# Cross-attention and a quantised FFN on one core: the last four row tiles in an order of their own, a second output bank, and the FFN weights in four transposing reads

## What is computed

```python
q = (layernorm(x) @ Wq).heads(); k = (ctx @ Wk).heads(); v = (ctx @ Wv).heads()
a = softmax(q @ k.T * 64**-0.5) @ v
x = x + a @ Wo + bo
def act_q(y, clip):                       # one scale for the whole tensor
    s = sigmoid(clip) * max(abs(y)) / 127
    return clip(round(y / s), -128, 127) * s
def w_q(w):                               # one scale for each row
    s = max(abs(w), axis=1) / 127
    return clip(round(w / s), -128, 127) * s
n  = act_q(layernorm(x), clip_x)
h  = act_q(silu(n @ w_q(w_gate).T) * (n @ w_q(w_up).T), clip_down)
x  = x + h @ w_q(w_down).T
```

## Time and profile before

| | |
|---|---|
| runs, us | 563.13, 563.48, 565.64; median 563.48 |
| profiled execution, us | 564.18; its span, first to last instruction: 562.4 |
| PE busy | 533.8 us (95% of the span) |
| PE weight loads, beside it | 354.2 us (63%) |
| DVE busy | 471.0 us (84%) |
| ACT busy | 293.3 us (52%) |
| POOL busy | 234.8 us (42%) |
| DMA | 93.82 MB, queue of SP 47.9% of 16 engines |

### The profile page before, as it was taken

One profiled execution on the slowest core, in us unless ns is written; L12 is line 12 of the kernel. 1 busy time (PEld: TensorE's weight loads), 2 busy tenths in 40 slices (PEclk: granted clock), 3 DMA queues, 4 the chain that ended last, 5 costly groups with the idle time before them and its releaser, 6 DMA issues.

```text
span 562.4 us, 7992 instructions
## 1 busy us (share of the span) xinstructions
PE 533.8 (95%) x2691; PEld 354.2 (63%) x2699; DVE 471.0 (84%) x874; ACT 293.3 (52%) x408; POOL 234.8 (42%) x352
## 2 busy tenths in 40 slices
PE   4999889999999999999789899999999999899997
PEld 1978668787888878787668644444444446343443
DVE  2747888999989898998987699999989988879883
ACT  3744546556555655544343555555554543999300
POOL 3576748769596876856542000000000000055441
PEclk9999999999999999999999999999999999999999
DMA  8717465765667574536294928750343130399987
GB/s 307 262 41 265 120 201 156 229 211 173 201 224 240 183 238 145 168 98 197 62 295 174 286 45 297 268 160 13 103 113 74 39 76 2 114 339 217 114 110 117
DMA packets 82338, 93.82 MB, mean 167 GB/s; under 512 B 46609, under 2 KB 49425, under 8 KB 82041
## 3 DMA queue, kind: packets, MB, share of 16 engines
q1 hardware_dynamic: 77973, 85.44, 47.9%
q0 software_dynamic: 4320, 7.87, 9.6%
q10 hardware_dynamic: 4, 0.00, 0.0%
HBM read 47.51 MB, written 37.78 MB: 152 GB/s over the span
## 4 chain that ended last, share of the span: by engine, by line
PE 46%; issue 34%; DVE 13%; DMA 5%; ACT 1%; POOL 1%; SPq 0%; POOLq 0%; DVEq 0%
PE QO L194 6%; PE QO L196 5%; PE QO L195 5%; PE SP L382 4%; PE WOP L495 3%; PE WOP L493 3%; PE WOP L494 3%; DMA out<-n2b 2%; PE PTP L1088 2%; PE QO L1088 2%; PE SP L1088 2%; PE PTP L430 2%; DVE P L401 1%; DVE mx L394 1%; DVE x L519 1%
## 5 line engine op out<-in xcount | busy, mean ns | idle before, releaser
L45 POOL DMA_DIRECT2D out<-n2b x30 | 30.2, 1039 | 213.8 <-DVE n2b L1099 213.8
L989 ACT ACTIVATE sil<-QO,fsc 128x512 f32<-128x512 f32 x88 | 60.5, 687 | 72.9 <-PE QO L983 72.9
L983 PE MATMUL QO<-nT,wgu 128*128 128x512 bf16 x352 | 90.4, 379 | 1.0 <-ACT nT L221 0.6
L983 PE MATMUL SP<-nT,wgu 128*128 128x512 bf16 x352 | 90.3, 379 | 0.0
L993 DVE SCALAR_TENSOR_TENSOR h<-SP,fsc,sil 128x512 f32<-128x512 f32 x88 | 65.9, 749 | 10.6 <-PE SP L983 10.4
L422 POOL TENSOR_TENSOR PN<-P,rs 128x512 f32<-128x512 f32 x64 | 44.3, 713 | 57.1 <-DVE rs L414 57.1
L996 DVE TENSOR_REDUCE hmx<-h 128x1 f32<-128x512 f32 x88 | 60.4, 686 | 3.0
L405 ACT ACTIVATE P<-P,r 128x616 f32<-128x616 f32 x32 | 25.9, 811 | 69.7 <-DVE P L401 69.7
L983 PEld LDWEIGHTS QO<-nT,wgu 128*128 128x128 bf16 x352 | 34.3, 98 | 42.7 <-DMA nT<-qb 1.1
L983 PEld LDWEIGHTS SP<-nT,wgu 128*128 128x128 bf16 x352 | 34.4, 98 | 41.5
L194 PE MATMUL QO<-xTs,wqs 128*128 128x512 f32 x128 | 52.0, 406 | 2.9 <-DVE xTs L225 2.6
(11 more groups left out here) (169 smaller groups left out, 1125.9 us busy)
## 6 DMA issues: line engine op xcount, KB each, us to landing
xTr<-in_xT SPq DMA_DIRECT2D x8, 1024.0 KB, 7.6
xn<-in_x SPq DMA_DIRECT2D x32, 256.0 KB, 3.8
out<-x SPq DMA_DIRECT2D x32, 256.0 KB, 2.9
n_rows<-n SPq DMA_DIRECT2D x32, 256.0 KB, 2.6
n2b<-n_rows SPq DMA_DIRECT2D x32, 256.0 KB, 3.9
out<-n2b POOLq DMA_DIRECT2D x30, 256.0 KB, 4.5
h_spill<-h SPq DMA_DIRECT2D x2, 2816.0 KB, 9.4
h<-h_spill SPq DMA_DIRECT2D x6, 768.0 KB, 8.0
```

Of the source, the lines that this page charges most:

```text
L983: m = e.matmul(ps, wv_[:, k, col:col + 128], nT[:, b % 2, :, k, :], start=(k == 0), stop=(k == 3))
L989: t_sil[n] = add("act", lambda e: e.activation(sil[:, n % SR, :], gp, ACT.Silu, scale=fsc[:, ic:ic + 1]), [t_g[n], t_fs, t_h.get(n - SR)] ...
```

## The change

- From step 28 on `attend` is no longer called. A function `last_batch` lists the work of tiles 28 to 31 in another order: `S(29)` and `S(30)` together, `S(31)` behind `wo(24)`, and `PT(30)` and `PT(31)` together. Row tile 30 has its scores and its transposes in `QO` instead of `SP` and `PTP`.
- Output tiles alternate between banks `WOP` and `MI`, in all batches; 30 and 31 use `PTP` and `SP`.
- The transposing read of the FFN weights is cut into four, each of 128 columns: two are listed behind step 27, two behind the loads of the last batch's values.
- The `dg` products go from DVE to ACT, behind `normed(26)`; their matmuls go behind `wo(31)`, into `QO`; the copy to `sdb` goes to ACT behind `normed(31)`.
- The first `keep_clock` has 8 matmuls instead of 20.
- `largest(24)` to `largest(29)` are listed two for each pass of the last loop.

```diff
+        def S_bank(n):
+            return QO if n == 30 else SP
         def S(n):
+            if n == 30:
+                free = [t_oss[6, 0], t_oss[6, 1]]
+            else:
+                free = [t_sub[29] if n == 31 else t_sub.get(n - 1)]
-            t_S[n] = add("pe", fn, [t_q[b], *t_kl, t_sub.get(n - 1)] + ...
+            t_S[n] = add("pe", fn, [t_q[b], *t_kl, *free], "S_mm")
...
         def PT(n):
+            free = t_sub[30] if n == 30 else t_pl[29] if n == 31 else t_pl.get(n - 1)
...
         def wo_bank(n):
-            return {28: PTP[:, 0:512], 29: SP[:, 0:512], 31: SP[:, 512:1024]}.get(n, WOP[:, :])
+            return {30: PTP[:, 0:512], 31: SP[:, 0:512]}.get(n, (WOP, MI)[n % 2][:, :])
         def wo(n):
-            free = t_x1.get(n - 1) if n < 28 else (t_pl[31], t_oss[7, 2], t_x1[27], t_oss[7, 3])[n - 28]
+            free = {30: t_pl[31], 31: t_oss[7, 2]}[n] if n >= 30 else t_x1.get(n - 2)
...
+        def load_wgu(k):
+            c.dma_turn(wgu[:, :].rearrange("p (k n) -> p k n", k=4)[:, k, :], wgud[:, k * 128:k * 128 + 128],
+                     [t_qh[7, 3], t_ws[24], t_ws[25]], "ld_wgu")
+        def last_batch():
...
+            PT(28)
+            S(29)
+            S(30)
+            PT_high(28)
+            soft_max(29)
+            soft_sub(29)
+            load_vb(7)
+            load_wgu(2)
+            load_wgu(3)
+            soft_exp(29)
+            soft_max(30)
+            soft_sub(30)
+            PT_low(28)
...
+            wo(24)
+            S(31)
...
+            wo(25)
+            residual(24)
+            PT(29)
...
+            wo(26)
...
+            PT(30)
+            PT_high(30)
+            PT(31)
+            PT_high(31)
...
+            wo(27)
+            residual(26)
+            PV_rest(7)
+            second(25)
+            residual(27)
+            largest(22)
+            for j in range(4):
+                PV(7, j)
+                if j == 0:
+                    normed(25)
+            second(26)
+            second(27)
+            largest(23)
+            normed(26)
-        for s in range(32):
+        for s in range(28):
             attend(s)
...
+            if s == 27:
+                load_wgu(0)
+                load_wgu(1)
+        last_batch()
...
         for n in range(28, NT):
             wo(n)
             normed(n - 1)
...
-            if n > 28:
-                largest(n - 2)
+            if n < 31:
+                largest(2 * n - 32)
+                largest(2 * n - 31)
...
+        t = add("pe", spread_scale, [t_dg, t_oss[7, 1]], "sd_mm")
+        t_sdb = copy("act", sdb[:, :], QO[:, 512:1024], [t], "sdb")
...
-            keep_clock(20 if which == 0 else 8)
+            keep_clock(8)
```

More of the change, by code:

```diff
@@ L832, in load_n2 @@
                 t_nl[b, tt] = dma("sp", n2b[:, b % 2, tt, :], n2d[4 * b + tt], waits, f"ld_n2b{b % 2}{tt}")
[L834 to L842, removed]
@@ L844, in block_kernel, with second @@
-        for s in range(32):
+        def load_wgu(k):
+            c.dma_turn(wgu[:, :].rearrange("p (k n) -> p k n", k=4)[:, k, :], wgud[:, k * 128:k * 128 + 128],
+                     [t_qh[7, 3], t_ws[24], t_ws[25]], "ld_wgu")
+        def last_batch():
+            def second(n):
+                second_stats(n)
+                second_aggr(n)
+                second_scale(n)
+            normed(22)
+            first_stats(31)
+            first_aggr(31)
+            first_scale(31)
+            wo(23)
+            residual(23)
+            PV_rest(6)
+            second(23)
+            for j in (2, 3, 0, 1):
+                PV(6, j)
+            PT(28)
[11 more added lines that the diff above has]
+            PT_low(28)
+            soft_exp(30)
+            normed(23)
+            soft_sum(29)
+            soft_rec(29)
+            soft_norm(29)
+            wo(24)
+            S(31)
+            soft_sum(30)
+            soft_rec(30)
+            soft_norm(30)
+            soft_max(31)
+            soft_sub(31)
+            soft_exp(31)
+            wo(25)
+            residual(24)
+            PT(29)
+            PT_high(29)
+            soft_sum(31)
+            soft_rec(31)
+            soft_norm(31)
+            PT_low(29)
+            wo(26)
+            residual(25)
+            second(24)
+            largest(21)
+            first_bias(31)
+            PT(30)
+            PT_high(30)
+            PT(31)
+            PT_high(31)
+            normed(24)
+            PT_low(30)
+            PT_low(31)
+            state["free"][0] = state["free"][1] = (t_pl[30],)
+            wo(27)
[12 more added lines that the diff above has]
+            normed(26)
@@ L849, in block_kernel @@
                 t_flat = [t_v[4], t_v[3], t_wol, ("qo_mm", c.count["qo_mm"])]
[L850 to L877, removed]
+            if s == 27:
+                load_wgu(0)
+                load_wgu(1)
+        last_batch()
+        t_wgu = ("ld_wgu", c.count["ld_wgu"])
+        gone = [t_S[31], t_q[7]]
+        for r in range(4):
+            dgt = wraw[:, 0, r * 128:r * 128 + 128]
+            t_dg = add("act", lambda e, r=r, dgt=dgt: e.activation(dgt, identF[:, :], ACT.Identity,
+                                                                   scale=wsc[:, 22 + r:23 + r]),
+                       [t_idF, t_wsc[25], t_wb[24], t_wb[25]], "dg")
         for n in range(28, NT):
@@ L891, in block_kernel, with spread_scale @@
         largest(31)
-        load_n2(1, gone[:2] + [t_n2s[4 + tt] for tt in range(4)])
+        load_n2(1, gone + [t_n2s[4 + tt] for tt in range(4)])
+        def spread_scale(e):
+            for r in range(4):
+                m = e.matmul(QO[:, 512 + r * 128:640 + r * 128], ones[:, :], wraw[:, 0, r * 128:r * 128 + 128],
+                             start=True, stop=True)
+            return m
+        t = add("pe", spread_scale, [t_dg, t_oss[7, 1]], "sd_mm")
+        t_sdb = copy("act", sdb[:, :], QO[:, 512:1024], [t], "sdb")
         add("act", lambda e: e.activation(warm[:, :], sge[:, :], ACT.Silu), [t_sge], "warm")
```

52 lines of the change are left out of this document (23 added, 29 removed).

## The result

| | before | after |
|---|---|---|
| median of 19 runs each, us | 563.48 (562.33 to 565.64) | 560.04 (557.22 to 562.35) |
| ratio, 95% interval | | 0.9935 (0.9923 to 0.9947) |
| profiled execution, us | 564.18 | 561.99 |
| its span, us | 562.4 | 560.2 |
| PE busy, us | 533.8 | 532.7 |

3.4 us faster, 0.65%; the forecast was 559.0, the range 557.0 to 561.5. The profiled execution of after lies near the upper end of its times, so its trace shows more of what went wrong than the median holds.

The account below looks back on a forecast made before the run. The prediction took PE, busy 95% of the span, as the bound, with DVE the nearer limit after the change. From the profiled 564.18, less 5.5 at the last residual, plus 1.0 for the clock, less 0.70: 559.0 us, range 557.0 to 561.5.

Parts of the forecast that it names:

- PE's side: Attention's last batch, scores of 29 to output tile 28: fewer stops and moved scale matmuls, output tile 28 6.7 us earlier.
- DVE's side: First softmax pass of tile 29 to the last residual: DVE becomes the nearer limit, leaving 5.5 us gained at residual 31.
- 1.0 late: At the residual of tile 28: DVE waits 2.2 us where 1.2 is free, and stays 1.0 us late to tile 31.
- the sign of a wrong main step: Scores of 30 start early as forecast, yet the residual of 31 comes less than 4 us earlier.
- The four reads: Weight reads on SP: 2.65 us for each quarter, no cost up to some 3.7 us for a quarter.
- the sign of being wrong on SP: The residual of tile 28 has a DMA in its bracket.
- The clock: Gap before the scale: PE stands still 3.1 us, a fall likelier than not, price 1.0 us within 0 to 3.5.
- The edits at nothing: `dg` on ACT, the copy to `sdb` on ACT and the second output bank: no cost or gain.
- The sum: Whole kernel: 564.18 - 5.5 + 1.0 = 559.7, less 0.70, 559.0 us; chance 0.50.
- the rival of the held clock: Gap before the scale: the clock doesn't fall, 563.48 - 5.5 = 558.0 us; chance 0.28.

Follow-up runs that it names:

- e6: e3 with the scores of tile 30 going to `SP` again instead of `QO`: 560.05 us, ratio 0.9938.
- e3: The changed kernel with 20 instead of 8 fillers before the scale and the last two reads behind the store of tile 27: 557.80 us, ratio 0.9899.
- e2: The changed kernel with the last two of the four reads listed behind the store of tile 27, 8 fillers kept: 560.24 us, ratio 0.9941.
- e1: The changed kernel with 20 instead of 8 fillers before the scale, nothing else: 557.92 us, ratio 0.991.
- e7: The kernel before with only the read of the weights cut into four: 563.47 us, ratio 1.0001.
- e4: The kernel before with 8 instead of 20 fillers before the scale, nothing else: 566.05 us, ratio 1.0038.
- e9: The changed kernel with 2 and 4 fillers behind the scale's transpose where 4 and 10 stood: 560.08 us, ratio 0.9946.
- e8: The kernel before with only the output banks alternating for row tiles 0 to 23: 562.83 us, ratio 0.9989.
- e5: e1 with the weights in one whole transposing read again, behind the loads of the last values: 558.43 us, ratio 0.9919.
- e10: e3 with 2 and 4 fillers behind the scale's transpose where 4 and 10 stood: 559.17 us, ratio 0.9932.

## Why the prediction was right, and where its terms were off

- **PE's side: right.** Output tile 28 was to come 19.6 after the scores of 29 and came 19.93; gain 6.35 for 6.7. The scores of 30 start 1.20 behind those of 29, without a bracket. e6 adds that the second score bank, which removes the stop at the scores of 30, is 2.1 of the 5.6. How the rest divides between the `dg` products taken from DVE, the paired transposes and the moved scale matmuls was not tried.
- **DVE's side: right with the store in time.** "1.0 late" is 0.98 in e3 (301.85 - 300.87), and the gain at the last residual 5.57 for the 5.5 taken. From tile to tile DVE then takes 2.71 (298.20 - 295.49), the 2.72 of the sum. In after's own profile the gain is 3.74, under the 4 that the prediction named as the sign of a wrong main step; e2, with only two reads moved, shows that the store made the difference.
- **The four reads, priced at nothing: too low in the profile.** The prices by size did not hold for quarters: 3.1 to 3.9 us each on the mean of a pair, not 2.65. In after's profile the store's lateness is the 1.75 us of the bracket of residual 28, and a DMA there was to be the sign of being wrong on SP; in e1's it is nothing. The step that failed is taking the price of a whole read as that of a piece, but that alone did not use up the margin: the four together took 14.30, 3.7 dearer than 10.59, where 4 were allowed. The rest of the margin went in terms that the prediction left out: the loads of the values took 10.40 for 9.32, a store of `normed` stands 0.6 ahead of tile 24's (290.11), and that store took 4.6 to land, not 4. The values were held up by 3.8 us and not by 1 (273.10 with the scores of 29 at 269.78; 270.62 and 271.08 before); PE did not wait for them. e7's ratio of 1.0001 says what the dearer quarters are worth where no one waits. The Trainium skill (DMA: Bandwidth & Descriptors, Rules for kernel authors) asks for a mebibyte or more in a transfer; 10.63 for one read against 13.03 to 14.30 for four agrees with it.
- **The clock: right that it falls, too cheap.** The stop with the store in time is 2.88 (3.1 forecast). The price was taken as 1.0 within 0 to 3.5; the profile has 2.22 against before's and 2.6 to 2.8 against those with a held clock, the medians of e1, e3 and e4 2.1, 2.4 and 2.5. What was mis-sized: I counted a part of the small matmuls, as the chain was "in part DVE's and DMA's". But the fillers stand ahead of the chain's own matmuls in PE's list, and at 1.2 GHz they need 0.87 and 1.70 us more (1.92 for 1.05, 4.20 for 2.50); with 0.41 to spare ahead of the transposes that alone is about the loss in the profile. They are most of the 3.9 us of small matmuls in the prediction, which did not tell them from the chain's own. e9 bears this out in part: without most of them 1.5 came back in this stage.
- **The edits at nothing** held: `dg` on ACT takes 1.27 for four, `sdb` 0.58. The second output bank is worth 0.4 to 0.6 by e8, which I had as nothing.
- **The sum.** 563.48 - 5.57 + 2.2, with up to 1.75 for the store, gives 560.1 to 561.9; the median is 560.04. The 1.2 by which the clock was priced too low is about the 1.04 by which the forecast missed; how much of the median is the store's was not measured, only that e2 without its wait is no faster. The runs of after show the branches: two with a mean granted clock of 0.999 took 557.22 and 557.99, which is the rival of the held clock (558.0); eleven at 0.996 to 0.997 took 558.9 to 560.6, and six at 0.993 to 0.994 560.0 to 562.35.
- **Left open:** the 0.6 us that the FFN takes longer in after; no experiment was aimed at it. It is not chance alone: the four profiles of kernels made from before have 242.1 to 242.6 and one wait of PE for the transposed rows (0.5 to 0.6), those made from after 242.6 to 243.1 (e9 and e10 aside) and two such waits, 1.0 to 1.2 in all. What makes the second wait is not shown.

## What to carry to other kernels

When work is brought forward, list what it will now meet: a store that was issued ten us ahead of its need (290.68 and 300.45 before) came within three of it, issued at the same time as ever (290.74). Fillers that keep TensorE's clock up are sized to a gap, so an edit that takes them away or widens the gap has to be priced with the granted clock on both sides of it, fillers included, because they stand in the same list as the chain. And when a version has run-to-run scatter, a look at which of its waits are near ties can pay more than the next reordering: e3 moves one pair of reads and lengthens one filler, and has both the best median and, in its four runs, a scatter of 0.02 us.

## What the runs showed of the hardware

The same stop may or may not bring the clock down. 1.95 us at the scores of 30 brought no fall in the profiles of before and e4, and one in those of e7 and e8 (low from 273.48 to 276.89 and from 274.02 to 277.43); 1.73 brought one in e6 and 1.98 in e5. From the one stop of 1.95 that I saw I had concluded that such stops are safe. In e10 no stop before the fall was longer than 1.03 (0.34, 1.03 and twice 0.56 behind `g_tr`). The Trainium skill (TensorE: Matmul & The Clock Gate, Why this matters for your kernels) warns of gaps longer than these; here shorter ones were enough. The fall may also come after the matmuls have started again, 1.2 us behind `g_tr` in e4. Its length differed with what PE did: 3.4 us in e4 to e8 and e10, where it came after the matmuls had started again and PE had full work; 6.8 in after and e2, where it came 0.7 and 0.8 us before they started; 10.2 in e9, where PE still had pauses of 1.30, 0.35 and 0.56.

A transposing read's time on SP was not fixed by its size: two quarters took 6.84 to 7.78 us ahead of the values and 6.12 to 6.52 behind them (e1, e7 and after), 7.39 and 7.83 behind the store of tile 27 (e2 and e3), and the whole read 10.6 in before, e5 and e8.
